# A convolution and window-attention block on one core: queries projected channel by channel, residual add and cubes on GpSimd, a new order on all engines

## The reference

```
x = x + dwconv3x3(x)                         # depthwise, with scale and bias
x = x + ffn(x)                               # 1x1 conv 64->128, relu, 1x1 conv 128->64
x = x + windowed_attention(x)                # windows of 7x7 pixels, image padded to 21x21
x = x + dwconv3x3(x)
x = x + ffn(x)
```

```
q = (relu(x wq) + 1e-6) / softplus(scale);  k = (relu(x wk + pos) + 1e-6) / softplus(scale);  v = x wv
focus(t) = t**3 * |t| / |t**3|               # norms over all 64 channels of a token
z = 1 / (q . sum_j k_j + 1e-6);  y = (q (k^T v)) z
y = y + depthwise 5x5 convolution of v inside the window;  output = y proj + bias
```

## Time and profile before

| | |
|---|---|
| median of 3 runs | 215.04 us (214.79 to 218.53) |
| the profiled execution | 217.01 us, its span 215.2 us, mean granted clock of PE 0.936 |
| busy | PE 164.2, DVE 121.2, ACT 94.3, POOL 42.1 us |
| PE idle ahead of L554, until `take_y` (L865) was done | 7.8 us |
| the same, until x2 (L840) was written | 6.5 us |

### The profile page before, as it was taken

The page is one execution under the profiler, slowest core; times in us unless marked ns, Lnnn a source line. Parts: engine busy times, 40 slices in busy tenths (PEclk is TensorE's granted clock), DMA queues, the critical chain, the costliest instruction groups (busy, mean ns, idle before and its releaser), DMA issues.

```text
span 215.2 us, 6346 instructions
## 1 busy us (share of the span) xinstructions
PE 164.2 (76%) x2728; PEld 77.4 (36%) x2728; DVE 121.2 (56%) x308; ACT 94.3 (44%) x160; POOL 42.1 (20%) x48
## 2 busy tenths in 40 slices
PE   0488877658777859798788466999589898898773
PEld 0112415235153535375164164635224233142110
DVE  1193478488585782983995895786116254513011
ACT  2044254735447656527517505772241423424311
POOL 3000153023211231151240233230300230300000
PEclk9999999997979996969969959999799999999999
DMA  6999956050000000000016003506207382645811
GB/s 154 257 265 203 214 92 144 4 123 17 3 5 0 3 3 3 3 3 5 0 52 140 3 9 89 97 29 147 74 4 178 109 189 83 157 141 148 189 49 49
DMA packets 18011, 18.49 MB, mean 86 GB/s; under 512 B 1088, under 2 KB 17728, under 8 KB 17984
## 3 DMA queue, kind: packets, MB, share of 16 engines
q1 hardware_dynamic: 17696, 17.70, 35.5%
q10 hardware_dynamic: 288, 0.39, 0.8%
HBM read 13.89 MB, written 4.19 MB: 84 GB/s over the span
## 4 chain that ended last, share of the span: by engine, by line
PE 43%; DVE 21%; issue 17%; ACT 11%; DMA 3%; POOL 2%; SPq 0%; DVEq 0%; ACTq 0%; POOLq 0%
PE ps L505 13%; PE ps L526 7%; PE ps L520 5%; ACT sq L382 3%; DMA xc<-in_x 3%; PE ps L688 3%; DVE nrm L798 3%; ACT hid L365 3%; DVE t L787 2%; PE ps L572 2%; PE ps L554 2%; DVE t L779 2%; ACT kvm L408 2%; PE ps L604 2%; ACT s L389 2%
## 5 line engine op out<-in xcount | busy, mean ns | idle before, releaser
L505 PE MATMUL ps<-xc,dwf 96*32 96x480 f32 (+1 forms) x384 | 48.0, 631 | 8.3 <-DMA xc<-in_x 8.3
L526 PE MATMUL ps<-hid,w2s 128*64 128x512 f32 x64 | 24.1, 675 | 7.2 <-ACT hid L365 7.2
L554 PE MATMUL ps<-wts,x 64*64 64x128 f32 x256 | 15.2, 331 | 14.7 <-DVE y L865 7.8
L505 PEld LDWEIGHTS ps<-xc,dwf 96*32 96x32 f32 x384 | 11.7, 116 | 36.7 <-issue 28.1
L322 POOL TENSOR_TENSOR vm<-vrest,cst 128x320 f32<-128x320 f32 x16 | 14.6, 932 | 49.1 <-ACT vrest L369 49.1
L520 PE MATMUL ps<-x,w1s 64*128 64x512 f32 x64 | 21.4, 751 | 2.4 <-ACT x L358 2.4
L365 ACT ACTIVATE hid<-ps,wts 128x512 f32<-128x512 f32 x32 | 20.2, 684 | 6.5 <-PE ps L520 6.4
L337 POOL TENSOR_TENSOR y<-y,fm 128x512 f32<-128x512 f32 x8 | 10.2, 1270 | 55.1 <-DVE y L865 43.7
L331 POOL TENSOR_TENSOR t<-sq,t 128x640 f32<-128x640 f32 x8 | 12.4, 1550 | 39.8 <-ACT sq L382 39.8
L358 ACT ACTIVATE x<-ps,wts 128x512 f32<-128x512 f32 x16 | 10.9, 682 | 21.0 <-PE ps L505 20.9
L834 DVE TENSOR_SCALAR x<-ps,bsum 128x512 f32<-128x512 f32 x8 | 6.0, 750 | 21.5 <-PE ps L526 21.5
(11 more groups left out here) (111 smaller groups left out, 252.1 us busy)
## 6 DMA issues: line engine op xcount, KB each, us to landing
xc<-in_x SPq DMA_DIRECT2D x16, 240.0 KB, 8.8
xc<-mid SPq DMA_DIRECT2D x16, 240.0 KB, 4.2
xc<-in_x SPq DMA_DIRECT2D x8, 256.0 KB, 7.2
mid<-x SPq DMA_DIRECT2D x8, 256.0 KB, 2.2
xc<-mid SPq DMA_DIRECT2D x8, 256.0 KB, 3.4
out<-x SPq DMA_DIRECT2D x8, 256.0 KB, 4.7
tab<-in_tables SPq DMA_DIRECT2D x1, 768.0 KB, 11.9
wts<-in_weights SPq DMA_DIRECT2D x1, 644.0 KB, 7.9
```

The costliest lines, as they stand in the source:

```text
L505: last = eng.matmul(out_ps[32 * q:32 * q + 32, :, :, to], dwf[:, s, q % 2, i, :], src[:, :, :, of], start=(i == 0), stop=False, skip_group ...
L526: last = eng.matmul(bank(m % 2)[64 * a:64 * a + 64], w2s[:, s, :], hid[:, m % 2, a, :], start=False, stop=True, skip_group_check=True)
L554: eng.matmul(bank(P_A + a)[64 * wx:64 * wx + 64, 128 * (2 * j + wy):128 * (2 * j + wy) + 128], x2[64 * a:64 * a + 64, g, j, at:at + 64], w ...
```

## The change

1. Queries. `query` multiplies wq (stationary) with x2 (moving, 256 tokens of both blocks), so q comes out with channels on partitions, as `attend` wants it. `turn_q` and its copy go. ScalarE squares q (`q_square`), GpSimd cubes it straight into `qt` (`cube_q`), ScalarE takes the sixth power (`q_sixth`). The sums over channels are then sums over partitions: `q_norms` multiplies each 64 tokens of q2 and of q6 with a column of ones, 40 products of one column. ScalarE copies these into `nrm`. The ratio and root of q of group g are taken together with those of k of group g+1 (`ratios`, `foc` has one place more).
2. GpSimd gets `third` (the residual add), the cube of k, `add_pads` and the small `geps`; its mask step becomes one instruction.
3. `key_value` splits in two parts and moves one slot later (g+3), on banks P_B and P_H; `qkv` splits into `query`, `kv_full` (P_A) and `kv_rest` (columns of P_H). Halves of the k tile only are reduced on VectorE.
4. The order: on PE the attention's products stand behind ffn1, and `attend` ahead of ffn2; on VectorE `take_y` comes in slot g+5, and `second` ahead of the k steps. The last groups' convolutions and feed-forwards interleave, and `project` of group 7 comes at the end of slot 13. The buffers of the key-value product are three instead of four, kf has two.

```diff
-            for n in range(SLOTS):          # PE
-                conv(m, n)
-                if 0 <= n - 7 < NG: project(n - 7, n)
-                if 0 <= n - 1 < NG: qkv(n - 1)
-                ffn1(m)
-                if 0 <= n - 2 < NG: turn_q(n - 2, n); key_value(n - 2)
-                ffn2(m)
-                if 0 <= n - 5 < NG: attend(n - 5, n)
-                if 0 <= n - 6 < NG: turn_y(n - 6, n)
+            for n in range(14):
+                if m is not None:
+                    conv(m, n)
+                if 0 <= n - 3 < NG:
+                    key_value_full(n - 3, n)
+                if 0 <= n - 7 < NG - 1:
+                    project(n - 7, n)
+                if m is not None:
+                    ffn1(m, n)
+                if 0 <= n - 5 < NG:
+                    attend(n - 5, n)
+                if n in FM_SLOT:            # {5: 0, 6: 2, 9: 3, 10: 5}
+                    window_conv(FM_SLOT[n], n)
+                    if m is not None:
+                        ffn2(m)
+                    if 0 <= n - 1 < NG:
+                        query(n - 1, n)
+                else:
+                    if 0 <= n - 1 < NG:
+                        query(n - 1, n)
+                    if 1 <= n < 5:
+                        kv_full(n - 1, n)
+                    if n >= 11 and n - 6 < NG:
+                        turn_y(n - 6, n)
+                    if m is not None:
+                        ffn2(m)
+                if n in FM_REST_SLOT:       # {5: 1, 9: 4}
+                    window_conv(FM_REST_SLOT[n], n)
+                if 0 <= n - 1 < NG:
+                    kv_rest(n - 1)
+                if 0 <= n - 3 < NG:
+                    key_value_rest(n - 3)
+                if 0 <= n - 2 < NG:
+                    q_norms(n - 2)
+                if 5 <= n <= NG:
+                    kv_full(n - 1, n)
+                if 6 <= n < 11:
+                    turn_y(n - 6, n)
+            project(NG - 1, 13)
+            conv(13, 14)
+            ffn1(13, 14)
+            conv(14, 15)
+            ffn2(13)
+            ffn1(14, 15)
+            ffn2(14)
+            conv(15, 16)
+            ffn1(15, 16)
+            ffn2(15)
...
+            def query(g, n):
+                eng.wait_ge(x2_ready, g + 1)
+                if 0 <= n - 3 < NG:
+                    eng.wait_ge(kvx_ready, n - 2)
+                for a in range(2):
+                    p = slice(64 * a, 64 * a + 64)
+                    last = eng.matmul(bank(P_B + 1)[p].rearrange("p (j n) -> p j n", j=GP), ww("wq")[p], x2[p, g, :, 0:PX], start=True, stop=True)
+            def kv_full(g, n):
+                eng.wait_ge(x2_ready, g + 1)
+                if g >= 1:
+                    eng.wait_ge(kfull_ready, g)
+                    eng.wait_ge(v_ready, g)
+                if 0 <= n - 5:
+                    eng.wait_ge(y_ready, n - 4)
...
+            def q_norms(g):
+                eng.wait_ge(q6_ready, g + 1)
+                one = cc("one")
+                for k, src in enumerate((q2[:, g % 2, :], q6[:, :])):
+                    for j in range(GP):
+                        for wy in range(2):
+                            for a, wx in QUADRANTS:
+                                p, h, at = slice(64 * a, 64 * a + 64), j ^ wx, NORM + 5 * k + 2 * wx + wy
+                                of = PX * j + place(wy, wx)
+                                eng.matmul(bank(P_H + a)[64 * h:64 * h + 64, at:at + 1], src[p, of:of + 64], one[p], start=True, stop=True)
...
             def ffn1(m, n):
                 eng.wait_ge(x1_ready, m + 1)
+                if 0 <= n - 4 < NG:
+                    eng.wait_ge(kvr_ready, n - 3)
+                if 0 <= n - 3 < NG:
+                    eng.wait_ge(qn_ready, n - 2)
+                if 0 <= n - 2 < NG:
+                    eng.wait_ge(vrest_ready, n - 1)
...
+            # GpSimd, slot n: add_pads(n-4), cube_k(n-2), v_masks(n-2), [n>=11: y_sum(n-6)], third(n-7),
+            #   q_guard(n-3), [n<11: y_sum(n-6)], cube_q(n-1)
+            # ScalarE, slot n: take_yt(n-7), take_kv_rest(n-4), take_q_norms(n-3), take_v_rest(n-2), k_square(n-2),
+            #   first(m), take_v_full(n-2), take_projected(n-7), k_sixth(n-2), hidden(m), root(n-2), take_fm,
+            #   [n>=11: take_yt(n-6)], q_sixth(n-2), q_square(n-1)
+            # VectorE, slot n: norm2(n-2), take_kv_full(n-3), norm6(n-2), ratios(n-2), k_focus(n-2), take_y(n-5),
+            #   q_first(n-1), [n<5: k_full(n-1)], second(m), k_rest(n-1), [n>=5: k_full(n-1)], k_guard(n-1)
-            # VectorE before: take_y(n-6), norm6(n-2), third(n-7), k_focus(n-2), k_raw(n-1), k_t(n-1), q_t(n-1),
-            #   take_kv_full(n-2), add_pads(n-2), norm2(n-1), cube_k(n-1), second(m)
```

More of the change, by code:

```diff
@@ L19 @@
 NB = 4
-KVB = 4
+QB = 4
+KVB = 3
 DX = [0, -1, 1]
@@ L76, in shape_constants @@
     put("sel")[:] = sel.reshape(128, 196)
+    put("one")[:] = 1
     tok = np.arange(128) % 64
@@ L387, in sixth @@
                 if g >= 1:
                     eng.wait_ge(ratio_ready, g)
[L389 to L396 removed]
+                eng.activation(k6[:, :], k3[:, :], ACT.Square).then_inc(k6_ready, 1)
@@ new lines, in q_square, with q_sixth @@
+            def q_square(g):
+                eng.wait_ge(q_ready, g + 1)
+                if g >= 2:
+                    eng.wait_ge(qn_ps, g - 1)
+                eng.activation(q2[:, g % 2, 0:GC], q1[:, :], ACT.Square).then_inc(q2_ready, 1)
+            def q_sixth(g):
+                eng.wait_ge(qt_ready, g + 1)
+                if g == 0:
+                    eng.wait_ge(zeroed, 3)
+                if g >= 1:
+                    eng.wait_ge(qn_ps, g)
+                eng.activation(q6[:, 0:GC], qt[:, g % QB, 0:GC], ACT.Square).then_inc(q6_ready, 1)
@@ L412, in take_fm @@
             def take_fm(e):
-                half, part, p0, p1 = FM_CHUNKS[e]
+                half, part = FM_CHUNKS[e]
                 eng.wait_ge(fm_ps, e + 1)
@@ L507, in conv, with ffn1 @@
                 last.then_inc(conv_ps, 1)
-            def ffn1(m):
+            def ffn1(m, n):
                 s = m // NG
@@ L560, in qkv, with kv_rest @@
-                for w, o in ((wkv, 320), (ww("wq"), 256)):
+                            last = eng.matmul(bank(P_A + a)[64 * wx:64 * wx + 64, 128 * (2 * j + wy):128 * (2 * j + wy) + 128],
+                                              x2[64 * a:64 * a + 64, g, j, at:at + 64], wkv[64 * a:64 * a + 64], start=True, stop=True)
+                last.then_inc(full_ps, 1)
+            def kv_rest(g):
+                eng.wait_ge(x2_ready, g + 1)
+                if g == NG - 1:
+                    eng.wait_ge(vrest_ready, g)
+                for a, j in QUADRANTS:
+                    last = eng.matmul(bank(P_H + a)[64 * j:64 * j + 64, REST:REST + 2 * C], x2[64 * a:64 * a + 64, g, j, WIN:WIN + 64],
+                                      wkv[64 * a:64 * a + 64], start=True, stop=True)
+                last.then_inc(rest_ps, 1)
@@ L566, in turn @@
+                last.then_inc(qn_ps, 1)
             def turn(out_ps, full, rest):
@@ L697, in setup @@
                     p = slice(64 * a, 64 * a + 64)
-                    last = eng.matmul(bank(P_A + 1)[p, 0:1], ww("proj")[p], ww("dwcb")[p], start=True, stop=True)
+                    eng.matmul(bank(P_A + 1)[p, 0:1], ww("proj")[p], ww("dwcb")[p], start=True, stop=True)
+                    last = eng.matmul(bank(P_A + 1)[p, 1:2], ewide[p, 0:C], cc("ident")[p, 64 * a:64 * a + 1], start=True, stop=True)
                 last.then_inc(setup_ps, 1)
-            for n in range(SLOTS):
+            for n in range(14):
                 m = conv_of(n)
@@ L937, in _ @@
                               cc("head_mask").unsqueeze(1).broadcast_to([128, 5, NH]), ALU.mult)
+            eng.tensor_copy(ecol[:, :], bank(P_A + 1)[:, 1:2])
             eng.tensor_tensor(projc[:, :], bank(P_A + 1)[:, 0:1], ww("projb"), ALU.add).then_inc(ones_set, 1)
+            eng.wait_ge(ones_set, 1)
             for n in range(1, SLOTS):
                 m = conv_of(n)
-                if 0 <= n - 6 < NG:
-                    take_y(n - 6)
+                if 0 <= n - 2 < NG:
+                    norm2(n - 2)
+                if 0 <= n - 3 < NG:
+                    take_kv_full(n - 3)
                 if 0 <= n - 2 < NG:
                     norm6(n - 2)
-                if 0 <= n - 7 < NG:
-                    third(n - 7)
+                if 0 <= n - 2 < NG + 1:
+                    ratios(n - 2)
                 if 0 <= n - 2 < NG:
                     k_focus(n - 2)
+                if 0 <= n - 5 < NG:
+                    take_y(n - 5)
                 if 0 <= n - 1 < NG:
-                    k_raw(n - 1)
-                    k_t(n - 1)
-                    q_t(n - 1)
+                    q_first(n - 1)
+                    if n < 5:
+                        k_full(n - 1)
+                if m is not None:
+                    second(m)
+                if 0 <= n - 1 < NG:
+                    k_rest(n - 1)
```

(11 more changed lines are left out.)

438 lines of the change are left out of this document (216 added, 222 removed).

## The result

The changed kernel takes 188.73 us (median of 3 runs, 186.80 to 193.43) beside 215.04: a ratio of 0.873 [0.862, 0.884]. Carried over to 215.04 us that is 187.8 us, 8.7 under the 196.5 forecast and just under the low end of 188. Two later measurements with five rounds each gave 0.895 [0.887, 0.903] (191.27 us) and 0.879 [0.870, 0.889] (190.43 us). Executions of one kernel fall into shorter and longer ones, and each ratio sets the shorter ones of both kernels side by side. So the change saves 10 to 13%, and 188 to 191 us is the kernel's time; no execution of the changed kernel (186.8 to 195.0) is as long as the shortest of the kernel before (210.5).

A forecast was written before the change was run, and what follows sets the result against it. A serial loop over four engines, none full, bounds the kernel. 19.6 (start) + 40.0 (slots 1 to 4) + (69.8 + 4.0 + 3.0) (5 to 9) + 28.3 (10 to 12) + 31.8 (last) = 196.5 us; range 188 to 209.

The forecast's parts named there:

- The wait for x2: PE ahead of the query products: the wait, 2.46 us in an early slot before, was counted as gone.
- Slots 10 to 12: No query work there: 11.7 us for slot 10 and 8.3 each for 11 and 12, sum 28.3.
- The last part: From slot 13 to the end: 31.8 us, with conv(14) waiting 1.5 us for its load.
- walked bare: Step-by-step sum for slots 5 to 9 before port and clock losses: 69.8 us, 14.0 of it for slot 7.
- the wait on `take_y`: PE ahead of `kv_full` in slot 7: `take_y` ends late, a new wait of 0.8 us.
- The port term: VectorE products with two SBUF inputs wait for GpSimd: 0.8 us a slot in slots 5 to 9 (4.0), 1.1 in 2 to 4.
- The norm products: PE, 80 one-column instructions summing q2 and q6: 1.6 us a slot, ends 1.75 and 4.0.
- Rival 3: Slots 2 to 9: the norm products run at 4.0 us instead of 1.6, giving 208 us; chance 0.10.
- The early slots: Slots 1 to 4: 38.9 us walked, 40.0 with 1.1 for the port.
- The middle slots: Slots 5 to 9, called the loss of the kernel before: 69.8 + 4.0 + 3.0 us after the change.
- The clock term: After the wait before `kv_full` PE runs partly at half clock: 0.75 us in each of four slots, 3.0.
- rival 2: PE becomes the bound and keeps its clock, GpSimd never in the way: 188 us; chance 0.12.

The follow-up runs named there:

- first execution: Profiled execution of the changed kernel in its first measurement (median 188.73 us); it took 193.43 us, span 191.6, clock 0.955.
- second execution: Profiled execution of the changed kernel run again with no edit (median 191.27 us); span 188.2, clock 0.98.

## Why the prediction was right in kind and 8 us too high

Against the execution with span 188.2, which ran at clock 0.98.

**Right.** The wait for x2 disappeared, and the gain came in the slots where it was forecast. Slots 10 to 12 are 28.4 for 28.3, by two misses that cancel: slot 10 takes 13.0 for 11.7 (y_sum waits for the copy of the last window part), slots 11 and 12 7.7 for 8.3. The last part is 31.1 for 31.8: conv(14) waited 0.17 us for its load in the one execution and not at all in the other, not 1.5, while conv(13) waited 0.88 for ScalarE's copy of the projection, which the forecast did not have.

**Right by luck.** Slot 7 took 14.1 for 14.0 walked bare, and the wait on `take_y` was 0.82 for 0.8. But PE reached `kv_full` at 10.4 after the slot's start, not 11.2, and `take_y` let it go at 11.3, not 12.0: both were walked some 0.7 too late. And the 14.1 holds the 0.79 that slot 8's first product waits for `yt`; `turn_y` itself was over at 13.4.

**The step that failed: the port on top of the path, and the length of the walk.** The forecast let the chain through `take_y` set all of slots 5 to 9 and put the port on top of it; PE's own list sets slots 5, 6 and 9, and the work in it was walked too long.

*The port term*, 4.0 in slots 5 to 9 and 1.1 before. In slot 8, the worst of the two slots in which PE waits for `take_y`, L917 took 0.40 for 0.18 and L924 0.90 for 0.82 (profile of the first execution):

```profile
108.14 0.40 DVE L917 TENSOR_TENSOR rat<-nrm,rat 128x20 f32<-128x20 f32 x1
...
108.83 0.90 DVE L924 TENSOR_TENSOR kf<-k,foc 128x640 f32<-128x640 f32 x1 [0.28 <-ACT foc L467]
109.13 0.69 POOL L351 TENSOR_SCALAR geps<-foc 128x10 f32<-128x10 f32 x1
```

With 0.1 on L964 that is 0.4 us, and 0.2 in slot 7, against 0.8. The longest such wait of slots 5 to 9 is in slot 6, where PE does not wait for `take_y` at all (second execution; free, it takes 0.16):

```profile
80.81 0.92 DVE L964 TENSOR_TENSOR den<-yr,geps 128x8 f32<-128x8 f32 x1
```

Slots 2 to 4 have none and slots 5 to 9 together 1.5, of which 0.6 lie on PE's path. So 0.6 of the 5.1 counted, and 1.27 us more GpSimd work in each of eight slots added nothing measurable. GpSimd waits as well: `geps` takes 0.69 here and 0.24 free (at 140.17). The Trainium skill, "SBUF — State Buffer", section "Who interferes with whom", has an exclusive lock; the trace agrees (the cube beside GpSimd's at 1.54 for 0.87 above), but what it costs the kernel is set by whether the one that waits has slack.

*The norm products*, 1.6 a group. Slot 2 has 35.99 to 37.21: 1.2, or 15 ns an instruction. In slots 2 to 4, where PE is the bound, that is 0.4 less in each, 1.2 in all; in 7 and 8 it only lengthens the wait. Rival 3 is refuted by this row. The Trainium skill's "TensorE: Matmul & The Clock Gate", section "LDWEIGHTS (loading the stationary operand)", prices one load of 64 columns at 53 ns, so an estimated 4.3 us for 80 one after the other; the trace does not agree with such a sum. One load's record lasts 135 ns (median of L660) and 80 of them with their products fit into 1.2 us, so the loads overlap. Whether it is the change of quadrant that lets them, no run separates.

*The early slots* came to 36.7 for 40.0: 1.1 port, 1.2 norms, and some 1.0 of small pieces, the wait of ffn1 for x1 among them: it was 0.81 in slot 2 and 0.2 in slots 3 and 4, less than I had walked. Slots 1 to 4 gave 14.2 of the 23.6 us between the profiled spans, though I had begun by calling the middle slots the loss.

*The middle slots* came to 72.9 for 76.8. Take out what the walk did not hold, 3.5 us of holes and 2.7 of half clock, and 66.7 is left for the 69.8 walked bare. The norms' 0.4 in slots 5, 6 and 9 is 1.2 of this 3.1; the rest is spread over the steps of the walk, as the 0.7 of slot 7 shows, and which of them were too long stays open. So the port's 4.0 and 3.1 of the bare walk were too much, and against them stands what I hadn't priced: holes of 1.7 and 1.2 us in two window parts (1.5 and 1.8 in the other execution) and one of 0.5 in `kv_full` of slot 5. The trace of before had such a hole, 2.8 us in L667.

```profile
65.22 1.27 PE L757 MATMUL ps<-vrest,tab 32*32 32x32 f32 x127
68.21 0.21 PE L757 MATMUL ps<-vrest,tab 32*32 32x32 f32 x1 [1.73 <-issue]
```

*The clock term*, 3.0. Slot 8 shows it at its dearest: after a wait of 2.03, `kv_full` takes 1.98 for 1.10 and `turn_y` 1.57 for 0.90, with its last pieces 1.8 us together.

```profile
112.89 1.98 PE L638 MATMUL ps<-wts,x 64*64 64x128 f32 x32 [2.03 <-DVE y L972]
114.81 1.57 PE L673 MATMUL ps<-cst,y 128*64 128x98 f32 x16
```

These two rows are of the execution with clock 0.955; the one with 0.98 has the same two durations, and its convolution of slot 9 takes 3.66 for 2.68, another 1.0. So the term is near 3 there (2.7), and some 5 in the other (slots 5 to 9 take 75.3 for 72.9); its size was right, its place (four slots alike) was not. After 0.82 us of wait in slot 7 the clock stayed full.

So the case that came about lies between the forecast and rival 2: PE is the bound in most slots, without GpSimd in the way, but it doesn't keep its clock and it waits for its instructions. That the total fell so near to rival 2's 188 is chance: unpriced holes and the clock took back what the bare walk had too much. I had given rival 2 0.12, though its ingredients (13.1 of PE work in a chain of 14) were in my own walk; the port and the clock term separated it from the forecast.

**What the parts are worth.** No single part gives the 24 us: the order of VectorE alone gains nothing, q's sums off VectorE give 4, the two GpSimd moves 3 to 5 each, the late query product some 5 in three slots, `second`'s place nothing. I infer, and no run shows it alone, that the rest comes from key-value a slot later, which turned 9.2 us of waits for k and q into none; that step was not undone by itself, as its banks and buffers hang on it.

## What to carry to other kernels

Look for the relay, not for the busiest engine: moving one link (`second` first) or thinning one (q's sums) moved the wait or was taken back, and only the whole new order, which gives most handovers the better part of a slot of cover, removed it. Price contention by who has slack, and if one such term separates two cases, give both a real chance. When a walk comes out right, compare its steps too: slot 7's length agreed while each step was 0.7 off. When products get small, PE can run out of instructions: look for idle time marked "issue" already in the trace of before, and put it into the sum.
